# Set-up of a graph kernel: edge arrays in rows of 2 KB, bit matrices made on the chip

## The reference, cut to what matters

```python
xn = _layernorm(x)
h = xn @ weight_l
msgs = edge_weight[:, None] * h[dst]
agg = jax.ops.segment_sum(msgs, src, num_segments=N)
x = x + (agg + bias_l + xn @ weight_r + bias_r) + attention(xn)
x = x + experts(_layernorm(x))      # 2 of 8 experts per node
```

## Time and profile before

| | us |
|---|---|
| median of 3 runs | 4451.65 (4448.86 to 4453.43) |
| the profiled execution, its own time | 4440.3 |
| its span | 4438.6 |
| mean granted TensorE clock | 0.864 of full speed |
| first scatter on POOL | 157.5 |

### The profile page before, as it was taken

How to read it: one execution, slowest core, us unless ns; L and a number is a source line. 1 busy time by engine, 2 the same in 40 slices (tenths; PEclk the granted TensorE clock), 3 DMA queues, 4 the chain that set the end, 5 groups by cost and what they waited for, 6 DMA issues and landing times. The chain is left out here.

```text
span 4438.6 us, 85552 instructions
## 1 busy us (share of the span) xinstructions
PE 3389.3 (76%) x16628; PEld 2802.7 (63%) x16629; DVE 2495.7 (56%) x11386; ACT 1685.6 (38%) x3095; POOL 3111.7 (70%) x2088
## 2 busy tenths in 40 slices
PE   1466666667677677878888888888758859999998
PEld 1355555555565555666666666666557758888887
DVE  3577777665555555666666666666548862222222
ACT  1233333344444443444444444444312224444443
POOL 0488888888888888888888888888855544444444
PEclk7788878788888888888888888888779979999999
DMA  9888888877777777777777777777789965565554
GB/s 380 241 146 155 152 148 147 157 117 118 116 109 115 116 113 114 102 108 108 105 104 107 108 103 105 108 107 102 91 217 296 294 187 143 139 145 141 141 140 114
DMA packets 588869, 638.95 MB, mean 144 GB/s; under 512 B 60524, under 2 KB 553156, under 8 KB 587138
## 3 DMA queue, kind: packets, MB, share of 16 engines
q0 software_dynamic: 279264, 269.84, 48.5%
q1 hardware_dynamic: 262234, 273.19, 20.9%
q10 hardware_dynamic: 47304, 95.18, 5.9%
HBM read 249.82 MB, written 390.09 MB: 144 GB/s over the span
## 5 line engine op out<-in xcount | busy, mean ns | idle before, releaser
L818 POOL DMA_INDIRECT agg<-msg,sidx x1664 | 2585.7, 1554 | 667.5 <-issue 408.7
L1122 PE MATMUL bank<-rows,Cmat 128*128 x3328 | 1025.7, 450 | 166.7 <-ACT msg L1315 140.6
L1315 ACT COPY msg<-bank 128x512 f32<-128x512 f32 x832 | 487.1, 585 | 1486.0 <-DMA agg<-msg,sidx 1209.8
L1122 PEld LDWEIGHTS bank<-rows,Cmat 128*128 128x128 f32 x3328 | 699.1, 224 | 346.7 <-issue 253.8
L873 DVE SCALAR_TENSOR_TENSOR sidx<-seen_sum,trash,srcf 128x4 int32<-128x4 f32 x416 | 92.7, 223 | 1022.8 <-DMA agg<-msg,sidx 1017.6
L2069 POOL DMA_INDIRECT out_dram<-x_y,x_node x210 | 325.7, 1551 | 473.1 <-issue 228.2
L856 DVE TENSOR_SCALAR Emat<-bank,srcf,wtf 128x128 f32<-128x128 f32 x1664 | 564.5, 398 | 0.0
L1106 PEld LDWEIGHTS bank<-Emat,pick 128*128 128x128 f32 x3328 | 518.3, 226 | 41.6 <-issue 17.7
L1106 PE MATMUL bank<-Emat,pick 128*128 128x128 f32 x3328 | 528.7, 311 | 1.6 <-DVE seen L860 1.6
L1097 PE MATMUL bank<-packed,both 128*128 (+1 forms) x416 | 187.3, 451 | 437.9 <-DVE seen L860 427.9
L860 DVE SCALAR_TENSOR_TENSOR seen<-bank,srcf,prior 128x128 f32<-128x128 f32 x1664 | 479.1, 341 | 0.0
(11 more groups left out here) (245 smaller groups left out, 4130.6 us busy)
## 6 DMA issues: line engine op xcount, KB each, us to landing
x_w<-in_L_ffn_W_dram SPq DMA_DIRECT2D x105, 512.0 KB, 4.1
agg<-expert_rows ACTq DMA_DIRECT2D x12, 4224.0 KB, 63.3
r_agg<-agg SPq DMA_DIRECT2D x196, 256.0 KB
x_zin<-table SPq DMA_DIRECT2D x105, 259.0 KB, 4.1
window_raw<-in_x_dram SPq DMA_DIRECT2D x208, 128.0 KB, 2.5
agg<-msg,sidx POOLq DMA_INDIRECT x1664
xn_rows<-n_xn ACTq DMA_DIRECT2D x49, 256.0 KB
xn_turned<-n_xnT ACTq DMA_DIRECT2D x49, 256.0 KB
```

The source lines that it names most:

```text
L818: pool.indirect_dma_start(scratch["agg"][r][:, :], bass.IndirectOffsetOnAxis(ap=sidx[:, j:j + 1], axis=0), msg[:, j % (2 * BATCH), :], Non ...
L1122: mm = nc.tensor.matmul(M[p][:, (q % 2) * D:(q % 2 + 1) * D], Cmat[:, b % 2, q, :], rows[:, bass.ds(slot, 1), :], start=True, stop=True)
L1315: nc.scalar.copy(msg[:, at:at + 2, :].rearrange("p q c -> p (q c)"), M[p][:, :]).then_inc(s_msg, 1)
```

## The change

The three edge arrays now come in rows of 512 edges (2 KB), four chunks in a partition: 4 tiles (`LTILES`), 3 of them whole (128 rows), the last with a rest of 31 rows and a short row of 20 edges. `dst`'s last tile is still loaded twice. PE transposes four blocks of 128 columns per tile, and the copies out of PSUM put column c of block r at chunk 4c + r (`chunks_of`, `turned_of`), with a stride of four. The six loads of `wide` and their wait are gone: DVE makes both halves of `wide` from `raw["src"]` by four masked copies, of which two cross from one half of the partitions to the other. The window plan now stands in three whole rows and a part of a fourth, so it moves in four small transfers instead of two. The memsets of the last tiles are 512 columns wide instead of 128.

```diff
-        raw = {k: sb(f"raw_{k}", [P, ETILES, P], dt) for k, dt in (("src", I32), ("dst", I32), ("wt", F32))}
-        flt = {k: sb(f"flt_{k}", [P, ETILES, P]) for k in ("src", "dst", "loc")}
+        raw = {k: sb(f"raw_{k}", [P, LTILES, LONG], dt) for k, dt in (("src", I32), ("dst", I32), ("wt", F32))}
+        flt = {k: sb(f"flt_{k}", [P, LTILES, LONG]) for k in ("src", "dst", "loc")}
...
         def load_edges(engine, to, a, done):
             engine.dma_start(to[:, 0:full_tiles, :],
-                             a[0:full_tiles * P * P].rearrange("(t c p) -> c t p", c=P, p=P)).then_inc(done, 16)
-            engine.dma_start(to[0:rest_rows, full_tiles, :],
-                             a[full_tiles * P * P:EFULL * P].rearrange("(c p) -> c p", p=P)).then_inc(done, 16)
...
+                             a[0:full_tiles * P * LONG].rearrange("(t c e) -> c t e", c=P, e=LONG)).then_inc(done, 16)
+            load_end(engine, to[:, full_tiles, :], a, done)
+
+        def load_end(engine, to, a, done):
+            engine.dma_start(to[0:rest_rows, :],
+                             a[full_tiles * P * LONG:BFULL * LONG].rearrange("(c e) -> c e", e=LONG)).then_inc(done, 16)
+            engine.dma_start(to[rest_rows:rest_rows + 1, 0:rest],
+                             a[BFULL * LONG:E].rearrange("(a e) -> a e", a=1)).then_inc(done, 16)
+
+        def chunks_of(to, i):
+            n = P if i < full_tiles else LREST
+            return to[:, i * LONG:i * LONG + n * BATCH].rearrange("p (c r) -> p r c", r=BATCH), n
+
+        def turned_of(bank, n):
+            return bank[:, :].rearrange("p (r c) -> p r c", r=BATCH)[:, :, 0:n]
...
-            sp.dma_start(scratch["base"].rearrange("(t w) -> t w", t=ETILES), wbase_i[0:ETILES, :]).then_inc(s_plan, 16)
-            sp.dma_start(scratch["general"].rearrange("(t w) -> t w", t=ETILES), ggen[0:ETILES, :]).then_inc(s_plan, 16)
-            sp.wait_ge(s_plan, 32)
+            for to, a, per in ((scratch["base"], wbase_i, LWINDOWS), (scratch["general"], ggen, LGROUPS)):
+                whole, left = full_tiles * per, LREST * per // P
+                sp.dma_start(to[0:whole].rearrange("(t w) -> t w", w=per), a[0:full_tiles, :]).then_inc(s_plan, 16)
+                sp.dma_start(to[whole:whole + left].rearrange("(a w) -> a w", a=1),
+                             a[full_tiles:LTILES, 0:left]).then_inc(s_plan, 16)
+            sp.wait_ge(s_plan, 64)
...
-            act.wait_ge(s_clear, 5)
+            act.wait_ge(s_clear, 4)
             load_edges(act, raw["src"], t["src"], s_src)
             load_edges(act, raw["wt"], t["edge_weight"], s_wt)
-            tiles, long_row = BFULL // SPAN, BATCH * P
-            for half in (0, SPAN):
-                act.dma_start(wide[half:half + SPAN, 0:tiles, :],
...
-            act.wait_ge(s_clear, 6)
+            act.wait_ge(s_clear, 5)
             for acc, n in clears[:READY]:
                 act.dma_start(clear_rows(acc, n), zeros).then_inc(s_zeroed, 16)
...
-                for four in FOURS:
+                for i in range(LTILES):
                     act.wait_ge(s_turn, n + 1)
-                    nc.scalar.copy(to[:, four[0] * P:(four[-1] + 1) * P], psum[n % 4][:, 0:len(four) * P]).then_inc(s_taken, 1)
+                    chunks, held = chunks_of(to, i)
+                    nc.scalar.copy(chunks, turned_of(psum[n % 4], held)).then_inc(s_taken, 1)
...
-            nc.vector.memset(wide[:, BFULL // SPAN:BTILES, :], 0).then_inc(s_clear, 1)
...
-            dve.wait_ge(s_wide, 96)
-            nc.vector.tensor_scalar(wide[0:SPAN], wide[0:SPAN], (P - 1) * P, None, ALU.bitwise_and).then_inc(s_masked, 1)
-            nc.vector.tensor_scalar(wide[SPAN:P], wide[SPAN:P], P - 1, None, ALU.bitwise_and).then_inc(s_masked, 1)
+            dve.wait_ge(s_src, 48)
+            upper, lower_half = raw["src"][0:SPAN], raw["src"][SPAN:P]
+            for to, bits in ((wide[0:SPAN], (P - 1) * P), (wide[SPAN:P], P - 1)):
+                nc.vector.tensor_scalar(to[:, 0:BTILES:2, :], upper, bits, None, ALU.bitwise_and).then_inc(s_masked, 1)
+                nc.vector.tensor_scalar(to[:, 1:BTILES:2, :], lower_half[:, 0:LTILES - 1, :], bits, None,
+                                        ALU.bitwise_and).then_inc(s_masked, 1)
...
-            for i in range(ETILES):
+            for i in range(LTILES):
                 last = nc.vector.tensor_scalar(flt["loc"][:, i, :], flt["dst"][:, i, :], tbase[:, i:i + 1], tfit[:, i:i + 1],
                                                ALU.subtract, ALU.mult)
...
+            for i in range(LTILES):
+                for r in range(BATCH):
+                    chunk = flt["loc"][:, i, r * P:(r + 1) * P]
+                    last = nc.vector.scalar_tensor_tensor(out=chunk, in0=edges["iota"][:], scalar=tgen[:, i:i + 1],
+                                                          in1=chunk, op0=ALU.mult, op1=ALU.add)
...
+            def turn_tile(bank, a, i):
+                for r in range(BATCH):
+                    mm = nc.tensor.transpose(bank[:, r * P:(r + 1) * P], a[:, i, r * P:(r + 1) * P], ident[:])
+                return mm
```

More of the change, by code:

```diff
@@ L39 @@
 BFULL = E // (BATCH * P)
-ETILES = CHUNKS // P
-EFULL = E // P
+LONG = BATCH * P
+LTILES = -(-CHUNKS // BATCH // P)
+LWINDOWS = P * BATCH // WINDOW
+LGROUPS = P * BATCH // CHUNK_GROUP
+LREST = CHUNKS // BATCH - (LTILES - 1) * P
 NACC = 4
@@ L48 @@
 assert NPAD <= P * P
-assert TILES % 2 == 0 and CHUNKS % P == 0 and CHUNK_GROUP % NACC == 0
+assert TILES % 2 == 0 and CHUNKS % BATCH == 0 and LREST % (CHUNK_GROUP // BATCH) == 0 and BTILES == 2 * LTILES - 1 and CHUNK_GROUP % NACC == 0
 CAP = 2 * P
@@ L160, in setup_phase @@
         s_wt = sem("setup_weight_loaded")
-        s_wide = sem("setup_wide")
         s_w = sem("setup_mix_weights")
@@ L178, in setup_phase @@
         block = ctx.enter_context(nc.Block())
[L179 to L183, removed]
+        full_tiles = BFULL // P
+        rest_rows = BFULL - full_tiles * P
+        rest = E - BFULL * LONG
+        assert full_tiles == LTILES - 1 and rest_rows < LREST
         WSPAN, WBAD, WPLAN, WLOCAL = 3, 11, 16, 21
@@ L221, in _ @@
             load_edges(sp, raw["dst"], t["dst"], s_dst)
[L222 to L225, removed]
+            load_end(sp, raw_end, t["dst"], s_dst)
             for to, a in weights:
@@ L332, in _ @@
             dve.wait_ge(s_pool, 3)
-            for i in range(ETILES):
-                last = nc.vector.scalar_tensor_tensor(out=flt["loc"][:, i, :], in0=edges["iota"][:], scalar=tgen[:, i:i + 1],
-                                                      in1=flt["loc"][:, i, :], op0=ALU.mult, op1=ALU.add)
+            for i in range(LTILES):
[3 more added lines that the diff above has]
+                                                          in1=chunk, op0=ALU.mult, op1=ALU.add)
             step(last)
@@ L345, in _ @@
             nc.vector.tensor_tensor(mix["bsum"][:], mix["bsum"][:], mix["brows"][:, 2, :], ALU.add)
-            for n, four in enumerate(FOURS):
-                dve.wait_ge(s_loc, n + 1)
-                nc.vector.tensor_copy(locf[:, four[0] * P:(four[-1] + 1) * P], psum[6 + n % 2][:, 0:len(four) * P]).then_inc(s_ltaken, 1)
+            for i in range(LTILES):
+                dve.wait_ge(s_loc, i + 1)
+                chunks, held = chunks_of(locf, i)
+                nc.vector.tensor_copy(chunks, turned_of(psum[6 + i % 2], held)).then_inc(s_ltaken, 1)
             nc.vector.tensor_tensor(edges["both"][:], ident[:, 0:SPAN], ident[:, SPAN:P], ALU.add)
@@ L380, in _, with turn @@
             turned = [0]
-            def turn(a, fours):
-                for four in fours:
+            def turn_tile(bank, a, i):
+                for r in range(BATCH):
+                    mm = nc.tensor.transpose(bank[:, r * P:(r + 1) * P], a[:, i, r * P:(r + 1) * P], ident[:])
+                return mm
+            def turn(a):
+                for i in range(LTILES):
                     n = turned[0]
@@ L387, in turn @@
                         pe.wait_ge(s_taken, n - 3)
-                    for i in four:
-                        mm = nc.tensor.transpose(psum[n % 4][:, (i - four[0]) * P:(i - four[0] + 1) * P], a[:, i, :], ident[:])
-                    mm.then_inc(s_turn, 1)
+                    turn_tile(psum[n % 4], a, i).then_inc(s_turn, 1)
                     turned[0] += 1
@@ L402, in _ @@
             pe.wait_ge(s_win, WLOCAL)
-            for n, four in enumerate(FOURS):
-                if n >= 2:
-                    pe.wait_ge(s_ltaken, n - 1)
-                for i in four:
-                    mm = nc.tensor.transpose(psum[6 + n % 2][:, (i - four[0]) * P:(i - four[0] + 1) * P],
-                                             flt["loc"][:, i, :], ident[:])
-                mm.then_inc(s_loc, 1)
+            for i in range(LTILES):
+                if i >= 2:
+                    pe.wait_ge(s_ltaken, i - 1)
+                turn_tile(psum[6 + i % 2], flt["loc"], i).then_inc(s_loc, 1)
```

(6 more changed lines are left out.)

48 lines of the change are left out of this document (19 added, 29 removed).

## The result

The changed kernel is slower: 4475.0 us, the median of six runs (4470.5 to 4479.1), against 4454.3 us for the kernel before, the median of six runs beside them. The ratio is 1.0045, with an interval of 1.0035 to 1.0055, some 20 us more. I had forecast 4,444 us, range 4,437 to 4,452, with a chance of 0.08 for slower.

What follows compares the result with a forecast made beforehand. POOL's scatters set the pace, the first held by set-up's DMA queue of loads and clears. Clears ending 7.7 us sooner took the 4,440.3 us run to 4,432.6 us; a 0.26% offset gave 4,444.0 us, range 4,437 to 4,452.

Steps and rivals of the forecast that it cites:

- part (5): Edge loads: 97 ns per 2 KB row (87 to 107), moving the clears' last end by -7.7 us (-9.6 to -5.7).
- part (2): Weight loads in set-up: unchanged, 1.44 MB by their shapes, 4.7 us at 305 GB/s.
- C: Rival, slower: 2 KB rows at 188 ns on the engine with 124 rest rows, 4,462 us; decides from 136 ns; chance 0.10.
- my 172 rows: Rows put ahead of DVE's start on one DMA engine: 172 x 0.087 us + 3.3 = 18.3 us.
- The late engine: Set-up loads: one DMA engine carries all 31-row rests, ending its loads at 27.0 us against 34.7 us before.
- D: Rival: rests spread or queues overlap fully, no late engine; `dst` there near 12 us; 4,437 to 4,441 us; chance 0.16.
- The gain of 7.7 us: Clears before the first scatter: their last end comes 7.7 us earlier, moving that scatter from 157.5 to about 149.8 us.
- Part (6): DVE's set-up chain and the messages: chain ends at 40.2 us against 46.6 us; message chain gains 5.7 us.
- the second step: DVE's set-up chain, after the subtraction: 16 for 13 of 0.27 us, 4.3 us.
- The cap by the messages: First scatters: POOL can gain at most the message chain's 5.7 us plus 2.8 us to spare, 8.5 us.
- the signs I had named for being wrong: First cast after 25 us, 2 KB rows over 136 ns, no one-engine tail, or POOL waiting for an early message.
- the message sign: First scatters: the forecast is wrong if POOL waits for a message among its first six scatters.

Runs made afterwards that it cites:

- late_weights: Kernel before, with SP's weight loads made to wait for ACT's first cast, so that they meet the clears: 4470.8 us, ratio 1.0044.
- hold: Changed kernel, with ACT waiting for all weights before it issues the first seven clears: 4447.7 us, ratio 1.0000 to the kernel before.
- wide_kept: Changed kernel, with the six loads of `wide` kept as before and masked in place: 4455.1 us, one run.
- hold_split: Changed kernel, with ACT waiting for the weights before the first clears and each 31-row rest loaded as 16 and 15 rows: 4429.8 us, ratio 0.9977.
- split: Changed kernel, with each 31-row rest loaded as 16 and 15 rows and no wait before the clears: 4435.3 us, one run.

## Why the prediction was wrong

**The step that failed** is the end of part (5): "Before, ACT came to them only at 24.54 us, behind the issues for `wide`, with the engines still full of loads; that delay cost nothing, and its end brings nothing." I had looked only at what the delay did to the clears. It was also what kept the clears off the engines until SP's fourteen weight transfers were through, or nearly (of SP's queue, which then also held the plan, 56 packets moved between 24 and 34 us, none from 34 to 45 us). The runs put in its place: the end of that delay costs 57 us of DVE's time and 16.8 us of POOL's. late_weights shows that the collision makes the loss, hold that taking it away gives back all of it at the first scatter, wide_kept (one run) that the removed issues were what had prevented it. The rests played their part: in hold, with no clear out yet, SP's issue of `wg` still took 7.56 us, and 1.08 us once the rests were spread, so the rests had made the weights late as well.

**With it fell part (2), "Weights stay".** I priced them by bytes: 1.44 MB at 305 GB/s, 4.7 us. The three columns have 3 KB between them and cost up to 60 us. The row that could have told me was there: in the earlier trace rows an expert load and other traffic share the engines, and packets are counted by queue; I asked it for the price of a row and not for who waits for whom. Nor did I name who waits for the weights. The code says it in one line, `dve.wait_ge(s_w, WEIGHTS)`, ahead of the copies that PE and ACT need; no rival had this wait, and C, which had the sign, placed the loss in the price of a row.

**Part (5), the price of a 2 KB row,** was near enough, though no run measured it by itself. DVE's first cast came at 15.9 us (forecast 18.3). Had all my 172 rows been through by then, a row took (15.9 - 3.3) / 172 = 73 ns; so the price was at or under the 87 ns of the earlier trace rows, or I had counted rows that weren't ahead. In neither case is it near the 136 ns from which C decides, and the last rows of 2 KB came at about 24 us, not 27.0 us.

**The late engine** is real: with the rests spread, and all else equal, the first scatter comes 8.5 us sooner (hold to hold_split), and 24.1 us sooner without the hold (changed to split), since the weights gain too. D is refuted for this kernel, where the rests aren't spread, and the spread, once written by hand, gave what D had promised: 144.9 us is 12.6 us before the 157.5 us, and DVE's first cast comes at 12.29 us in hold_split, where D had put `dst` (near 12 us).

**The gain of 7.7 us** was there in part, but for the collision: hold has its first scatter 4.2 us before and 5.6 us before the second run of the old kernel. In its whole time it doesn't show (ratio 1.0000). Its clears go out at 26.88 us, no sooner than before (24.54 and 26.70 us), and from there to the first scatter it takes 126.5 us, against 133.0 and 132.3 us: the shorter loads are worth 6 to 7 us of that stretch. That the wait for the weights ate the rest is argued, not shown.

**Part (6), DVE's chain,** held in its sum, 39.45 us against 40.2 us, and partly by luck: it started 2.4 us sooner than forecast and took 1.6 us longer. In its terms, the masks took 5.9 us, not 4.1 (1,536 elements of 64 partitions took 1.75 us, 2,048 took 1.22 us), the subtraction 1.9, not 2.6 us, the second step 4.29, not 4.3 us. The cap by the messages was right: in hold and hold_split the third scatter waits 1.60 us for its message, with all clears done. And of the signs I had named for being wrong one came true: POOL waited for a message among its first six scatters.

**What would have shown it in time:** I had written what to look for on DVE's first cast and on POOL's first scatters, and nothing for the weights; the message sign says that set-up is late, not why. The check that was left out is the list of every wait in front of the step that sets the end, each with its own latest time.

## What to carry to other kernels

When an edit frees an issuing engine early, ask what it will now issue, and what is still unfinished on the other queues at that moment: count pieces, not bytes, and price each at the duration of the largest piece it alternates with. Load small scattered operands first, or hold the big store until they are in, and check that a rest of rows isn't carried by one engine: 31 rows were here, 16 and 15 weren't. An accidental delay can be the only thing that keeps an order.

## What the runs showed of the hardware beyond that

- Packets of two queues took turns one for one: 288 to 288 between 60 and 80 us, with sizes of 4 bytes and 33.8 KB, and 2 and 2 in 2 us on a single engine at 90 us.
- An issue can hold its engine for long: SP 16.4 us for one row of 1 KB in the changed kernel (0.32 us in hold), ACT 37 us for twelve clears (7.1 us for seven). Each time much on that queue had not landed yet. That a limit on outstanding pieces is behind it is argued, not shown.
- DVE's masking took longer for fewer elements: 1.75 us for 64x1536, 1.22 us for 64x2048. The slower form reads partitions 64 to 127 and writes the odd tiles, the faster one reads 0 to 63 and writes the even ones. Whether the result went to the same half of the partitions or the other made no difference (1.22 and 1.22 us, 1.75 and 1.75 us), and partitions 64 to 127 aren't slow to read by themselves: in the kernel before, 64x3584 took 2.02 us in place in either half. What is left is the place and the odd number, three, of the tiles written; neither was tried alone.
